# Scores and product with the values ahead of the first head's turned weights in a fused decoder kernel

## What is computed

```python
x = x + attention16(ctx, ctx, layernorm(x), mask1)   # 16 heads of 32
x = x + ternary_ffn(layernorm(x))                    # 512 -> 2048 -> 512
x = x + attention8(layernorm(x), ctx, mask2)         # 8 heads of 64
x = x + mixture_of_experts(layernorm(x))
```

```python
energy = einsum('nqhd,nkhd->nhqk', q, k)
attn = softmax(where(mask == 0, -1e20, energy) / sqrt(D), axis=3)
out = einsum('nhqk,nkhd->nqhd', attn, v).reshape(N, L, E) @ Wo + bo
```

## Time and profile before

| | |
|---|---|
| median of 3 runs | 1915.18 us (1915.1 to 1916.68) |
| the profiled execution's own time | 1915.71 us |
| its span, first to last instruction | 1914.0 us |
| TensorE busy, share of the span | 98% |
| VectorE, ScalarE, POOL busy | 67%, 54%, 42% |
| mean granted TensorE clock | 0.999 of full |

### The profile page before, as it was taken

How to read it: one execution, slowest core, us unless ns; L and a number is a source line. 1 busy time by engine, 2 the same in 40 slices (tenths; PEclk the granted TensorE clock), 3 DMA queues, 4 the chain that set the end, 5 groups by cost and what they waited for, 6 DMA issues and landing times.

```text
span 1914.0 us, 42677 instructions
## 1 busy us (share of the span) xinstructions
PE 1878.9 (98%) x13700; PEld 1443.8 (75%) x13700; DVE 1286.6 (67%) x3985; ACT 1032.5 (54%) x2674; POOL 797.8 (42%) x1482
## 2 busy tenths in 40 slices
PE   6999999999999999999999999999999999999999
PEld 5888888888888644444447888888888877788876
DVE  5887877666677678788875565655656566544476
ACT  5767767777777644544444444444444453222243
POOL 3454555656555545655542232222322233222254
PEclk9999999999999999999999999999999999999999
DMA  6334434433443777665663212122121237222131
GB/s 233 135 138 136 135 113 151 156 135 123 146 143 110 136 157 195 172 147 134 140 146 112 79 57 100 67 88 78 55 99 68 76 114 240 99 82 74 66 132 46
DMA packets 221533, 230.32 MB, mean 120 GB/s; under 512 B 123441, under 2 KB 139825, under 8 KB 221377
## 3 DMA queue, kind: packets, MB, share of 16 engines
q1 hardware_dynamic: 221376, 228.42, 39.1%
HBM read 144.47 MB, written 56.64 MB: 105 GB/s over the span
## 4 chain that ended last, share of the span: by engine, by line
PE 89%; DVE 3%; SPq 2%; DMA 2%; issue 2%; POOL 1%; ACT 1%; POOLq 0%; DVEq 0%; ACTq 0%
PE bank L1172 19%; PE bank L1158 18%; PE bank L2739 13%; PE bank L1228 8%; PE bank L1868 8%; PE bank L1243 6%; PE bank L1211 5%; PE bank L1913 4%; PE bank L1148 2%; DMA b_hqT<-b_hq 1%; SPq L1450 1%; PE bank L2636 1%; SPq L1456 1%; PE bank L2778 1%; DVE m_hrow L2555 0%
## 5 line engine op out<-in xcount | busy, mean ns | idle before, releaser
L582 POOL TENSOR_SCALAR a_probs<-a_probs,a_rinv 128x256 f32<-128x256 f32 x512 | 237.4, 482 | 269.6 <-DVE a_rinv L933 269.6
L711 ACT ACTIVATE a_probs<-a_probs,a_negm 128x256 f32<-128x256 f32 x512 | 254.6, 502 | 95.9 <-DVE a_negm L917 94.8
L582 POOL TENSOR_SCALAR c_probs<-c_probs,c_rinv 128x256 f32<-128x256 f32 x128 | 67.0, 533 | 371.6 <-DVE c_rinv L933 371.6
L917 DVE CUSTOM_DVE_ANT_0 a_probs<-bank,a_mbias 128x256 f32<-128x256 f32 x512 | 191.7, 417 | 7.3 <-PE bank L1211 6.6
L2739 PE MATMUL bank<-m_xnT,m_s 128*128 128x512 f32 x768 | 184.4, 391 | 0.0
L926 DVE COPY a_pT<-bank 128x512 f32<-128x512 f32 x128 | 88.3, 690 | 134.8 <-PE bank L1228 134.7
L711 ACT ACTIVATE c_probs<-c_probs,c_negm 128x256 f32<-128x256 f32 x256 | 127.0, 500 | 75.0 <-DVE c_negm L917 75.0
L2739 PEld LDWEIGHTS bank<-m_xnT,m_s 128*128 128x128 f32 x768 | 142.6, 188 | 30.5 <-issue 0.8
L1228 PE MATMUL bank<-a_ident,a_probs 128*128 128x128 f32 x1024 | 154.9, 274 | 4.0 <-ACT a_pT L719 2.3
L1228 PEld LDWEIGHTS bank<-a_ident,a_probs 128*128 128x128 f32 x1024 | 122.0, 141 | 23.6 <-issue 10.8
L1730 ACT ACTIVATE b_hq<-b_hround 128x1024 bf16<-128x1024 f32 x64 | 67.2, 1052 | 123.4 <-POOL b_hround L1669 119.0
(11 more groups left out here) (287 smaller groups left out, 4318.9 us busy)
## 6 DMA issues: line engine op xcount, KB each, us to landing
kept<-a_cT SPq DMA_DIRECT2D x32, 512.0 KB, 5.2
m_ew<-in_L_ffn_w_dram SPq DMA_DIRECT2D x24, 512.0 KB, 8.5
a_cbuf<-in_ctx_dram SPq DMA_DIRECT2D x16, 512.0 KB, 5.6
a_xbuf<-in_x_dram SPq DMA_DIRECT2D x16, 512.0 KB, 4.8
a_resb<-in_x_dram SPq DMA_DIRECT2D x16, 512.0 KB, 4.1
b_part<-in_L_ffn_w_gate_dram SPq DMA_DIRECT2D x32, 256.0 KB, 3.0
b_part<-in_L_ffn_w_up_dram SPq DMA_DIRECT2D x32, 256.0 KB, 4.0
b_part<-in_L_ffn_w_down_dram SPq DMA_DIRECT2D x32, 256.0 KB, 4.3
```

The lines of the kernel that those rows point to most:

```text
L582: last = nc.gpsimd.tensor_scalar(pr, pr, rinv[:, s, r:r + 1], 0.0, ALU.mult, ALU.add)
L711: nc.scalar.activation(pr, pr, ACT.Exp, bias=negm[:, s, h % 2, t:t + 1], scale=-1.0, accum_out=ssum[:, s, QT * (h % 2) + t:QT * (h % 2) + ...
L917: nc.vector.tensor_tensor_reduce(out=probs[:, s, h % 2, t], in0=s_bank[h][:, t * SEQ:(t + 1) * SEQ], in1=mbias[:, el.par], scale=-sm_scale ...
```

## The change

On TensorE's queue, scores of the next quad and the product with the values of the quad before go ahead of the transposes of the first head in phase a too; the totals stay around the scores. On VectorE's queue the copy of the first head's turned weights goes behind the first head's scores, and the low halves of the slot before go ahead of these scores in every quad (that was so in quad 1 only).

```diff
@@ def quad_of_16(el, q), VectorE @@
             ne, nq = next_quad(el, q)
             more = nq > 0 or el.has(1)
-            probs_out(el, q, 0)
             if beside:
                 beside.vector_scales(dve, el, q)
             recip(el, q, 1)
             if q == 2 and filled(el):
                 rows_out(dve, but_one, 1)
             lows_of_slot_behind(el, q, 2)
-            if q == 1:
-                lows_of_slot_behind(el, q, 3)
+            lows_of_slot_behind(el, q, 3)
             if more:
                 scores_out(ne, nq, 0)
-            if q != 1:
-                lows_of_slot_behind(el, q, 3)
+            probs_out(el, q, 0)
             if more:
                 scores_out(ne, nq, 1)
@@ def iteration(el), TensorE @@
-                    if j == 0 and QUADS == 2:
-                        if nq > 0 or el.has(1):
-                            scores(ne, nq)
-                        probs_v_before(el, q)
-                    transpose_probs(el, q, j)
-                    if j == 0 and QUADS == 4:
-                        if beside and beside.totals_at(el, q):
+                    if j == 0:
+                        if beside and QUADS == 4 and beside.totals_at(el, q):
                             wait_for(pe, otlo_done, el.n * QUADS + q - 1)
                             beside.tensor_totals(pe)
                         if nq > 0 or el.has(1):
                             scores(ne, nq)
-                        if beside and beside.totals_at(el, q):
+                        if beside and QUADS == 4 and beside.totals_at(el, q):
                             beside.tensor_totals_read(pe)
                         probs_v_before(el, q)
+                    transpose_probs(el, q, j)
```

## The result

The changed kernel takes 1924.93 us (median of 4 runs, 1924.12 to 1928.9), the one before beside it 1915.93: a ratio of 1.0046, with a 95% interval of 1.0034 to 1.0058, so 9 us or 0.46% slower. The forecast was 1922.3 (+7.1) in a range from 1917.3 to 1926.5. The four runs of the kernel before (1915.10 to 1918.79) were good ones: in the four later sessions its median over 11 to 21 runs was 1918.3 to 1919.0, and the changed kernel was not run beside those. Against them its loss would read 5.9 to 6.6 us, so the whole time alone does not fix the size of the effect to better than 3 us.

The account below looks back on a forecast made before the run. TensorE, busy 98% of the span, was taken as the bound. Terms +8.4 - 1.5 - 1.1 + 1.3 = +7.1 us gave 1922.8 from the profiled 1915.7, stated as 1922.3 us, range 1917.3 to 1926.5.

Parts of the forecast that it names:

- Step 1: Quad 0, elements 1 to 14: second head's transposes wait 0.60 us for VectorE's copy of the first's; +8.4 us.
- Step 2: Changed neighbours of scores, products and transposes on TensorE's queue make shape changes cheaper, 0.10 us an element; -1.5 us.
- Step 3: Quad 0: the 0.08 us wait ahead of unit o0 for VectorE's low half of q1 goes, 14 times; -1.1 us.
- Step 4: Element 15 and turn to next phase: empty first slots stall TensorE 2.0 us, 0.7 hidden by a DMA wait; +1.3 us.
- The faster one: Rival: in quad 0 the first head's copy is back before tc0 ends, no new stall; 1910.2 us, 5%.
- VectorE was not late: Rival: VectorE reaches the first head's copy 0.3 us late each time, +4.2 us, to 1926.5; 17%.
- Nothing large was given back: Rival: the quad 0 stall is real but mostly absorbed by later waits, +3.4 us, 1918.6; 13%.

Follow-up runs that it names:

- the new version: Changed kernel with last element in old order, half of o0 moved into quad 0's first slot, o0's rows added earlier: 1913.41 us, ratio 0.9980; again 0.9985.

## Why the prediction was right

**Step 1** held to the hundredth: turnaround 1.53, wait 0.60 from the starts, 14 times; the experiments with quad 0 alone (+8.2) and with a second short slot (+7.7) show the cause. VectorE was free in time, by 0.1 (its copy starts at 441.90, the last of the first head's scores began at 441.43 and takes 0.34 to the next), where the text had 0.04.

**Step 2** was sized too large. S behind the units of 256 columns costs 1.60 us from start to start (437.69 to 439.29) against the 1.52 ahead of a T: the 0.08 that was taken from the 8-head phase. Quad 2 saves 0.06, quad 3 only 0.02, and quad 1 loses 0.02 where 0.01 was to be won, which makes -0.75 over 14 elements; quad 0 has 8.25 for the 8.4 of step 1, so -0.15. Together that is -0.9 for -1.5, with whatever step 3 gave in it. By the rule on drains from the Trainium skill (TensorEngine Tiling (Array Packing), Key Properties), with three changes of mode in either order, the term would have been nothing. The trace lies between the two.

**Step 3 failed.** It took the 0.44 from T1 to o0 in rows 3 for every element. The trace of before has it in 3 of 14 elements; the other eleven look like this one:

```profile
76.97 0.60 PE L1228 MATMUL bank<-a_ident,a_probs 128*128 128x128 f32 x4
77.32 0.96 PE L1158 MATMUL bank<-a_wo,a_oT 128*128 128x512 f32 x3
```

0.35, no wait. The saving was 3 x 0.08 = 0.2, and a T that restarts from a wait takes 0.38 to its follower in place of 0.36, which gives that back. The step's -1.1 was 0. The wait was large only where the step did not count it, in element 15: there it is 0.85 from T1 to o0 before and 0.38 after.

**Step 4** had 2.0 on the queue and 0.7 hidden; it was 2.5 and 0.6. By quads it is +0.6, +1.0, +0.9 and -0.1. T1 of quads 0, 1 and 2 comes 1.53 after T0, 1.04 late each, as forecast. In quad 0 the 0.47 of the wait ahead of o0 comes off. In quad 1 there is a wait that the text did not have: S stands 0.49 us for the scores' read-out (651.04). Before, T0 stood between T3's unit and S, for 0.56 us (642.64 to 643.20), and there was no wait; that this is the reason is read from the order and was not tested.

Corrected, the sum is 8.4 - 0.9 + 0 + 1.9 = 9.4, less 0.1 of element 0, where 9.2 is the shift in the trace at 690 us. The three errors (0.6, 1.1 and 0.6) all lie on the same side, so the number did not come out by errors that cancel. The profiled execution has a further 1.7 behind that point, which the last section tells.

**The rivals.** The faster one is excluded by the same 1.53. VectorE was not late in elements 1 to 15; it was in element 0, where T1 follows T0 after 2.44 us, at no cost to the queue. Nothing large was given back. That T0's own cover was the question, and not drains, is shown by quads 1 to 3, which keep the new order at no loss.

## What to carry to other kernels

With one PSUM bank passed through another engine, the work between its two uses has to be at least the turnaround (here 1.53 us: 0.69 from the transposes' start to the copy's, 0.69 copy, 0.15 back); before moving long work away from between two uses, find the shortest filler that stays. An order moves with its partner: VectorE's half of this change alone cost 5 us and TensorE's 86, and each move of a unit needs a walk down the queue of the engine that frees its bank, for a waiting instruction ahead of ready work. A per-element saving read from one element must be looked up in a second one before it is multiplied by fourteen.

## What was not expected of the hardware

In the profile of the changed kernel TensorE stands idle from 688.1 to 690.4 us for the transposing DMA, and right behind, from 690.8 on, runs for 3.4 us at a granted clock of 0.50 of full, which is 1.2 GHz:

```profile
688.10:690.40 2.30, 0.00 (x0) 0.00 (x0) 2.27 (x5) 0.00 (x0) 1.36 (x4) 1.00 1.14 232
690.80:694.20 3.40, 3.40 (x10) 1.22 (x9) 0.22 (x2) 1.06 (x1) 2.21 (x2) 0.50 0.39 86
```

The columns are the stretch, its length, the busy time of the matmul side, the weight load, VectorE, ScalarE and POOL (with the number of instructions), the granted clock, the DMA share and GB/s. The 16 products take 5.13 us from start to start of their neighbours (690.49 to 695.62) where before they took 3.45 (681.25 to 684.70): 1.7 us more. Twelve of the fourteen profiles of this case have a stretch at 0.50 here, with a wait of 2.3 to 3.9 us. The two without are those of the kernel before: it idled 3.03 and 3.64 us at this place and kept the full clock, while the new version idled 3.04 in one profile and fell to 0.50 a little later. So the idle time alone does not decide it; what does was not found. The kernel before has its stretch elsewhere, in element 0 (41.5 to 44.9 us), behind a wait of 1.87 us and from inside one of 0.90, and the changed kernel has one there too. The 1.7 is a fifth of the effect under study. VectorE's work of the next phase shows it: it stands 10.9 us later than before up to 790 us, and 9.4 later from 825 to 930 us, so most of it is given back in later waits, and the end of the span is 9.7 later.
